# A two-layer gated cross-attention kernel: loops written out, waits on climbing counts, and one weighing moved behind the next fill

## The reference

```python
# layer 0: attention without projections, 16 heads of 16
x = x + g * softmax(ln(x) @ ctx^T * 0.25) @ ctx        # per head
y = fp8_gemm(ln(x), kernel) + bias                     # x and kernel rounded to float8
x = x + g2 * y
# layer 1: attention with projections and a mask
q, k, v = ln(x) @ Wq.T + bq, ctx @ Wk.T + bk, ctx @ Wv.T + bv
s = where(mask == 0, -1e9, q @ k^T / 4)                # per head
x = x + g * (softmax(s) @ v @ Wo.T + bo)
z = ln(x) * gamma + beta
scale = max(|z|) / 127                                 # over all batches
x = x + g2 * (round(z / scale) * scale) @ ternary(w).T
```

## Time and profile before

| what | us |
|---|---|
| median of 3 runs | 2161.66 |
| lowest and highest | 2160.32, 2164.04 |
| span of the profiled execution | 2160.4 |
| first pass, steady stretch | about 63 to 766 |
| change-over of the passes | about 766 to 864 |
| second pass, steady stretch | about 864 to 2005 |
| third pass | about 2065 to 2157 |

### The profile page before, as it was taken

One profiled execution on the slowest core, in us unless ns is written; L12 is line 12 of the kernel. 1 busy time (PEld: TensorE's weight loads), 2 busy tenths in 40 slices (PEclk: granted clock), 3 DMA queues, 4 the chain that ended last, 5 costly groups with the idle time before them and its releaser, 6 DMA issues. The chain is left out here.

```text
span 2160.4 us, 72530 instructions
## 1 busy us (share of the span) xinstructions
PE 1939.2 (90%) x23712; PEld 1392.2 (64%) x23712; DVE 1806.1 (84%) x3446; ACT 1650.1 (76%) x2631; POOL 1337.8 (62%) x2676
## 2 busy tenths in 40 slices
PE   3898888989889986999999999999999999999757
PEld 2666666666666664666666666666666666666445
DVE  4689999999999987888888888888888888888379
ACT  1788888888888884777777777777777777777479
POOL 2688888888888874455555555555555555555300
PEclk9999999999999998999999999999999999999689
DMA  2222222222222210000000000000000000000035
GB/s 79 68 70 66 66 66 66 69 67 66 68 66 66 67 41 15 24 22 21 22 22 22 22 22 20 20 22 22 22 22 22 20 20 22 22 22 15 1 122 189
DMA packets 113868, 95.20 MB, mean 44 GB/s; under 512 B 13440, under 2 KB 113792, under 8 KB 113792
## 3 DMA queue, kind: packets, MB, share of 16 engines
q1 hardware_dynamic: 113792, 94.23, 14.2%
HBM read 60.63 MB, written 33.55 MB: 44 GB/s over the span
## 5 line engine op out<-in xcount | busy, mean ns | idle before, releaser
L892 DVE TENSOR_REDUCE a_nmax<-bank_max 128x8 f32<-128x1024 f32 x512 | 623.0, 1217 | 92.1 <-DVEq L891 91.0
L1174 PE MATMUL bank_exp<-UM,U 32*128 32x256 f32 x4096 | 558.6, 390 | 3.4 <-PEq L1325 3.4
L687 ACT ACTIVATE probs<-bank_exp 128x1024 f32<-128x1024 f32 x256 | 262.3, 1025 | 274.5 <-ACTq L686 274.5
L1189 PE MATMUL bank_o<-probs,V 128*17 128x128 f32 x8192 | 326.4, 276 | 102.4 <-PEq L1185 95.7
L1174 PEld LDWEIGHTS bank_exp<-UM,U 32*128 32x128 f32 x4096 | 373.5, 185 | 6.4 <-issue 5.5
L1189 PEld LDWEIGHTS bank_o<-probs,V 128*17 128x17 f32 x8192 | 192.1, 96 | 258.2 <-issue 257.3
L985 DVE CAST bank_max<-mask_b 128x1024 f32<-128x1024 bf16 x256 | 314.3, 1228 | 23.0
L610 ACT ACTIVATE probs<-bank_exp 128x1024 f32<-128x1024 f32 x256 | 262.4, 1025 | 61.0 <-ACTq L609 45.8
L1167 PE MATMUL bank_max<-UM,U 32*128 32x256 f32 x2048 | 294.9, 405 | 4.7 <-PEq L1200 2.6
L1167 PE MATMUL bank_max<-UM 32*128 32x256 f32 x2048 | 290.2, 400 | 9.1 <-PEq L1279 6.0
L680 ACT ACTIVATE bank_exp<-sh_T 128x1024 f32<-128x1024 bf16 x256 | 264.0, 1031 | 0.6 <-ACTq L693 0.4
(11 more groups left out here) (170 smaller groups left out, 4625.2 us busy)
## 6 DMA issues: line engine op xcount, KB each, us to landing
X<-in_x SPq DMA_DIRECT2D x128, 128.0 KB, 2.1
ctx<-in_ctx SPq DMA_DIRECT2D x128, 128.0 KB, 2.0
out_y<-U SPq DMA_DIRECT2D x128, 128.0 KB, 1.7
ctx<-out_y SPq DMA_DIRECT2D x128, 128.0 KB, 2.0
out_y<-X SPq DMA_DIRECT2D x64, 256.0 KB, 2.1
mask_i<-in_mask_BxSxS_ik SPq DMA_DIRECT2D x128, 64.0 KB, 1.7
X<-in_L_xattn_Wq SPq DMA_DIRECT2D x1, 256.0 KB, 2.8
X<-in_L_xattn_Wk SPq DMA_DIRECT2D x1, 256.0 KB, 3.3
```

The lines of the kernel that those rows point to most:

```text
L687: nc.scalar.activation(a_probs[n], exp_pair[:, :, :, :].rearrange("p i h t -> p (i h) t"), ACT.Exp, scale=SCALE).then_inc(act_own, 1)
L892: return v.tensor_reduce(a_nmax[:, k2, n * H // 2:(n + 1) * H // 2], max_pair[:, :, :, :].rearrange("p i h t -> p (i h) t"), axis=AX.X, op ...
L1174: last = mm(exp_pair[:, r % 2, 2 * c:2 * c + 2, :], before[0][32 * r:32 * r + 32, c, :], before[1][32 * r:32 * r + 32, c, :, :], start=Fal ...
L1189: last = mm(bank_o[32 * j:32 * j + VW, (2 * c + n) * P:(2 * c + n + 1) * P], V[k4][:, 8 * c + 2 * r + e, :], a_probs[n][:, r % 2 * HG + 2 ...
```

## The change

The loops are gone: every step of all passes is straight-line code, on every engine. Every semaphore now only climbs, and each wait is for a number known when the program is built; no consumer lowers anything. The semaphores got new names, one set for each pass. What an engine used to signal with an instruction of its own behind a wait for itself, the producing instruction signals now. Waits for things that are certain already were left out, and several waits ahead of a group of matmuls are spread over its first ones.

In the first pass three orders differ. TensorE weighs half 0 of batch `i - 3` behind the first fill of step `i`, where it used to weigh half 0 of batch `i - 2` at the end of step `i`; the transposes of the attention sums follow the transposes of inputs and maxima and the FP8 product, right ahead of the second fill. ScalarE copies `bank_o` behind the exponential of half 1 instead of at the end of the step. VectorE takes the reciprocal and scales the attention behind its other statistics and the FP8 rounding, right ahead of the second maximum. In the second pass the order of the engines' work stays.

The core of the diff, cut:

```diff
-        def steps(run, lo, hi, first, last, engine, close=lambda: None):
...
-            with engine.Fori(first, last - UNROLL + 1, UNROLL) as i:
-                for k in range(UNROLL):
-                    run(i + k, (first + k) % UNROLL, lambda off: True)
-                close()
+        def both_passes(run_a, run_b, settle=lambda: None):
+            for i in range(A_LO, A_ALONE):
+                step_of(run_a, i)
+                if i < 13:
+                    settle()
...
# ScalarE, first pass
                 if live(-2):
-                    exp_pair_of(1)
+                    act.wait_ge(a_scores, 2 * (i - 2) + 1)
+                    exp_of(1).then_inc(a_probs_made, 1)
+                if live(-3):
+                    act.wait_ge(a_attn_made, i - 2)
+                    attn_copy().then_inc(a_attn_out, 1)
                 if live(1):
...
-                if live(-2):
-                    copy_attn()
# ScalarE, second pass
                 if live(-2):
-                    exp_settled(0)
+                    act.wait_ge(b_scores, 2 * (i - 2) + 2)
+                    exp_of(0).then_inc(b_probs_made, 1)
                 if live(-3):
-                    act.wait_ge(cn_T, 1)
-                    act.sem_inc(cn_T, -1)
+                    act.wait_ge(b_cn_Td, i - 2)
...
                     if live(-2):
-                        probs_settled()
+                        act.wait_ge(b_probs_made, 2 * (i - 2) + 2)
# VectorE, first pass, behind the statistics and the FP8 rounding
+                if live(-3):
+                    vec.wait_ge(a_attn_back, i - 2)
+                    mine(v.reciprocal(rden[:, :], bank_oh[:, :, DH]))
+                    settle()
+                    attn_scaled().then_inc(a_attn_normed, 1)
+                if live(0):
+                    vec.wait_ge(a_max_scores, 2 * i + 2)
+                    max_of(1, k % 2).then_inc(a_max_made, 1)
# TensorE, first pass
+            def fill_a(i, n, k, live):
...
+                if live(-2):
+                    if n == 1:
+                        pe.wait_ge(a_probs_made, 2 * (i - 2) + 1)
+                    elif live(-3):
+                        pe.wait_ge(a_probs_made, 2 * (i - 3) + 2)
+                    add_shift(n, k % 2, True, i + 1 if live(0) and n == 0 else 0)
...
             def step_a(i, k, live):
-                fill(0, now, before, k % 2)
-                if live(-3):
-                    attn_transpose()
+                fill_a(i, 0, k, live)
+                if live(-3):
+                    for c in range(DC):
+                        for j in range(HG):
+                            last = weigh((k + 1) % RING, 0, c, j)
+                    last.then_inc(a_attn_made, 1)
                 if live(1):
...
+                if live(-3):
+                    pe.wait_ge(a_attn_out, i - 2)
+                    attn_transposes().then_inc(a_attn_back, 1)
+                fill_a(i, 1, k, live)
...
-                if live(-2):
-                    weigh_pair((k + 2) % RING, 0).then_inc(attn_made, 1)
# TensorE, second pass, weighing of half 0
-                    weigh_pair((k + 2) % RING, 0).then_inc(attn_made, 1)
-                if live(1):
-                    pe.wait_ge(v_out, 1)
-                    pe.sem_inc(v_out, -1)
+                            if c == 0 and j == 0:
+                                pe.wait_ge(b_probs_made, 2 * (i - 2) + 2)
+                            if live(1) and c == 0 and j == 1:
+                                pe.wait_ge(b_v_out, i + 2)
+                            if live(1) and c == 0 and j == 2:
+                                pe.wait_ge(b_masked, i + 2)
```

More of the change, by code:

```diff
@@ L273, in build @@
-        stored = [sem(f"stored{n}") for n in range(RING)]
-        def steps(run, lo, hi, first, last, engine, close=lambda: None):
-            def outside(i):
-                run(i, i % UNROLL, lambda off: 0 <= i + off < NB)
-                close()
-            for i in range(lo, first):
-                outside(i)
-            with engine.Fori(first, last - UNROLL + 1, UNROLL) as i:
-                for k in range(UNROLL):
-                    run(i + k, (first + k) % UNROLL, lambda off: True)
-                close()
-            for i in range(last, hi):
-                outside(i)
@@ L303, in xs, with steps_c @@
+        def steps_c(run, lo, hi):
+            for i in range(lo, hi):
+                run(i, i % RING, lambda off: 0 <= i + off < NB // 2)
         def xs(b):
[L304 to L306 removed]
+            return X[:, b * D:(b + 1) * D]
         def xs2(b):
[L309 to L315 removed]
@@ L435, in _ @@
+            for n in range(RING):
+                sp.wait_ge(stored[n], 16 * (NB // 2 // RING))
         @block.gpsimd
@@ L910, in step_a @@
[L910 to L924 removed]
+                    vec.wait_ge(a_max_scores, 2 * i + 1)
@@ new lines, in step_a @@
+                    max_of(0, k % 2).then_inc(a_max_made, 1)
+                if live(5):
+                    vec.wait_ge(*x_landed(i + 5))
+                    n_bn = a_stat_of(v.bn_stats(st6[:, :], xs(i + 5)))
+                if odd and (live(5) or live(-3)) and (live(1) or live(-7)) and not live(0):
+                    vec.wait_ge(a_stats_got, (i + 1) // 2 + 1)
+                if live(5):
+                    vec.wait_ge(a_stats, n_bn)
+                    a_stat_of(v.bn_aggr(a_stat[:, s, 2 + n, :], st6[:, :]))
@@ L1183, in weigh_pair @@
[L1183 to L1192 removed]
+                return last
@@ new lines, in add_shift, with max_mm @@
+            def add_shift(n, ring, start, masked=0):
+                for r in (2 * (1 - n), 2 * (1 - n) + 1):
+                    if r == 3 and masked:
+                        pe.wait_ge(a_masked, masked)
+                    last = mm(exp_pair[:, r % 2, :, :], ones_b[32 * r:32 * r + 32, :],
+                              sh_T[ring][32 * r:32 * r + 32, :], start=start, stop=False, skip_group_check=True)
+                return last
+            def max_mm(r, c, now, start):
+                return mm(max_pair[:, r % 2, 2 * c:2 * c + 2, :], now[0][32 * r:32 * r + 32, c, :],
+                          now[1][32 * r:32 * r + 32, c, :, :], start=start, stop=True, skip_group_check=True)
@@ L1221, in step_a @@
+                    last.then_inc(a_in_Td, 1)
                 if live(-1):
-                    pe.wait_ge(shift_made, 1)
-                    pe.sem_inc(shift_made, -1)
+                    pe.wait_ge(a_shift_made, i)
+                    if odd and live(-9) and not live(1):
+                        pe.wait_ge(a_fq_out, (i - 9) // 2 + 1)
                     for b in range(4):
```

1018 lines of the change are left out of this document (421 added, 597 removed).

## The result

The changed kernel takes **2103.04 us** (median; 2099.47 to 2105.06), the one before beside it 2161.57 (2160.32 to 2164.04). The ratio is 0.9726, 95% interval 0.9711 to 0.9741: 2.7% faster. I had predicted 2120, range 2090 to 2152. The profiled execution's span went from 2160.4 to 2097.7 us, and the program from 72530 instructions to 57564.

The account below looks back on a forecast made before the run. It took the wait chain between engines to bound the first pass and TensorE with its waits the second. Savings of 32 (second pass), 7 (first pass) and 3 (edges) made 42 us less: 2120, range 2090 to 2152.

Parts of the forecast that it names:

- main case: Whole kernel: shorter links and direct signal save 32 + 7 + 3 us, giving 2105 to 2132; chance 0.5.
- the case in which the links all but vanish: Rival, whole kernel: busy queues hide even the setup's 0.05 us a link; 63 us less, 2098; chance 0.11.
- Part 1: All passes: without decrements, each link into TensorE shortens by 0.06 us and each into ScalarE by 0.08.
- Part 3: First pass: half 0's weighing moves behind the next first fill; step 5.86 against 5.908 us, 7 us less.
- VectorE did not take over: Rival, first pass: VectorE's serial work becomes the bound, step near 6.05 us, 2143 in all; chance 0.24.
- Part 2: Second pass: exponential starts sooner and signals half 0's probabilities directly; 0.26 us a step, 32 us less.
- The lower bound of the term: Second pass: only the direct signal helps, exponential to weights load 0.23 to 0.11 us; 15 us less.
- set-up, change-over and tail: Outside the passes' steps: some 40 links in series, 0.07 us each, 3 us less.
- Part 4: Written-out loops: a longer program is charged nothing; loop turns cost 0.2 us each, 2.7 us in the first pass.
- The rival by the skill: Whole kernel: decrements nearly free, links stay long, accumulator's copy makes first-pass step 6.13 us; 2173; chance 0.09.

Follow-up runs that it names:

- the kernel with the extra instructions: Changed kernel plus one meaningless semaphore instruction behind each wait of the chain on TensorE and ScalarE, in both passes: 2164.91 us, ratio to before 1.0016.

## Why the prediction came out as it did

**What came out.** The time, 2103, lies in the range (2090 to 2152), 17 us below the 2120 that I named and just under the band of the main case (2105 to 2132). It is near the 2098 of the case in which the links all but vanish, but that is not what happened: there a first-pass step was to be 5.72, and it is 5.857. The mechanism is that of the main case; what is missing from its sum is below.

**Right, with numbers.** Part 1: a link with nothing between wait and work is 0.06 long into TensorE (forecast 0.05) and 0.08 to 0.09 shorter into ScalarE. Part 3: 3.48 and 2.38 against 3.44 to 3.47 and 2.41, a step of 5.857 against 5.86, 7.4 us against 7; copy and list bind where I said. VectorE did not take over: it is busy 644.73 of 720 us and the step is no longer than the chain gives.

**Partly luck, the 7 us of Part 3.** It is the difference of two larger terms, and both were sized too small: the new order with long links was to cost 26 us over the pass and costs 30.3 (780.99 us from the 1st to the 128th copy in the kernel with the extra instructions, 750.69 before), the shorter links were to give 33 back and give 37.8 (780.99 to 743.24). The two misses cancel.

**Mis-sized, Part 2.** The term was 0.26 a step; 0.30 was measured on TensorE, and 0.01 of loop turn. The missing 0.04 is mostly the 0.03 between load and first matmul that a decrement leaves (table), which I had not counted. The lower bound of the term, 0.12 for the direct signal with the other decrements left in, held: a step is 9.084 with the direct signal and 9.20 without it. But what makes up this 0.12 is not the place of the signal: raised behind the wait and the copy, with no decrement near, it costs 0.04. The rest of the 0.18 that went between exponential and weights was two more semaphore instructions, the one behind ScalarE's wait for itself and the one behind TensorE's. The mechanism of the sum was right: semaphore instructions.

**Missed, the edges.** For set-up, change-over and tail I had 3 us less (40 links of 0.07). Set-up and change-over gave 3.5 and the stretch behind the last copy 2.4, but the last steps of the second pass gave 12, for which there was no term. They make up most of the difference between the 42 forecast and the 62.7 between the spans (58.5 between the medians). The earlier trace rows has this in one digit: a granted clock of 0.99 over 1080 us. I read it as full speed; it was 30 us at 0.50. The step of the sum that failed is this one: the end of the second pass was costed by links, and 8.3 us of what it took before hung on the clock. That the changed kernel's clock fell less far was not foreseen, and why it did is open; its waits there are hardly shorter.

**Not asked.** The prediction priced the move of the weighing and the shorter links as one term of 7 us. The rows at hand give the case that I did not work out, the old order with short links: by the even step of the earlier trace rows, 2.63 - 0.14 + 2.55 - 0.14 + 0.72 = 5.62. That it is close to the measured mean, 5.595, is chance: the even step is 5.38 and the odd one 5.81. The step of the earlier trace rows stands at a loop's turn, so its 0.72 is too long; in the step before it of the same parity the weighing takes 0.59 (393.16 to 393.75), which gives 5.49. For the same reason the prediction's 5.90 met the mean of 5.908 by chance; ordinary even steps of before take 5.79 and odd ones 5.98. The move costs 34 us that the links paid for, and a version without it beats the changed kernel by 33 us.

**Part 4.** That a longer program costs nothing held to 0.1% for the kernel before, but the 0.2 us a turn did not come back: other stalls took their place. The Trainium skill, "Runtime: NRT & Kernel Launch", section Instruction fetch mechanics, says that a taken branch can force a fetch stall and that kernels prefer full unrolling, this being one reason; the kernel written out alone, at 1.0014 (1.0002 to 1.0027), shows no gain from it.

**The rival by the skill.** If semaphore instructions were nearly free, as the Trainium skill's "Advanced Engine Details and Errata", section DMA Bandwidth Details, lets one expect, the kernel with the extra ones would have stayed at 2103. It took 62 us more. That page of the Trainium skill has its figure, about one cycle, among those of DMA and may mean another increment than an engine's own instruction. Another page of the Trainium skill fits the runs better: "Perfetto Trace Analysis", section Per-engine timelines, has an instruction decoded and put in a wait queue, where it stands ready while its semaphore is awaited; my reading is that with a separate instruction behind the wait, the work is made ready only after it. The 0.06 to 0.09 a link agree with this in sign; that it is the cause was not isolated.

## What to carry to other kernels

On a chain that crosses engines, put the wait directly ahead of the instruction that does the work and let the producing instruction raise the signal: each semaphore instruction in between cost 0.06 to 0.09 us a link here, 62 us over the 256 steps of both passes. When one edit shortens the links and another moves work, work out all four combinations; here the move cost 34 us that the other edit hid. And look at the granted clock in windows of a few us where a pipeline runs empty, not over the whole pass.

## What the hardware showed that I had not expected

- Adding 18 matmuls that compute nothing made the kernel before 10 us faster (0.995, 0.9931 to 0.9969), because TensorE's clock stayed at 1.00, where it had fallen to 0.50 in steps with waits of up to 1.95 us. In the changed kernel, with waits of up to 1.86 us, it fell only to 0.87 in the mean.
- In single steps of the kernel before written out, an idle ScalarE started its exponential 0.79 us behind the start of the matmuls that it waited for instead of 0.51; what held it is open.
- A decrement behind TensorE's wait also puts 0.03 us between the first weights load and its matmul; without it they start together.
